# Products that nobody reads in TensorE's queue of an attention and experts kernel

## What is computed

```python
xn = _layernorm(x, axis=-1)
x = x + attn(xn, w_attn, w_proj) + ffn(xn, gate_w, gate_b, expert_bias, w1, b1, w2, b2)

# attn: 16 heads of 16, phi(a) = elu(a) + 1, causal, chunk by chunk of 128 rows
q, k, v = split(xn @ w_attn.T)
scores = where(tril, phi(q) @ phi(k).T, 0)
num = scores @ v + phi(q) @ S            # S: the sum of phi(k).T @ v of the chunks before
den = scores.sum(-1) + phi(q) @ z
y = num / (den + 1e-06);  attn = y @ w_proj.T

# ffn: each row goes to one of 8 experts
top_idx = argmax(xn @ gate_w.T + gate_b + expert_bias)
h = relu(xn @ w1[e] + b1[e])             # 256 -> 1024
y = h @ w2[e] + b2[e]                    # 1024 -> 256
```

## Time and profile before

| | |
|---|---|
| median of 3 executions | 514.7 us (514.43 to 514.87) |
| the profiled execution | 514.6 us |
| its span, first to last instruction | 512.8 us |
| mean granted clock of TensorE | 0.984 |
| TensorE products busy | 479.5 us, 94% of the span |
| VectorE, ScalarE, GpSimd busy | 406.6, 280.6, 259.5 us |
| longest waits of TensorE | 6.6 us for the first squared weights, 5.3 us for the first gathered rows |

### The profile page before, as it was taken

How to read it: one execution, slowest core, us unless ns; L and a number is a source line. 1 busy time by engine, 2 the same in 40 slices (tenths; PEclk the granted TensorE clock), 3 DMA queues, 4 the chain that set the end, 5 groups by cost and what they waited for, 6 DMA issues and landing times.

```text
span 512.8 us, 17442 instructions
## 1 busy us (share of the span) xinstructions
PE 479.5 (94%) x6067; PEld 393.1 (77%) x6067; DVE 406.6 (79%) x881; ACT 280.6 (55%) x537; POOL 259.5 (51%) x469
## 2 busy tenths in 40 slices
PE   1899999999999999999987599999999999999996
PEld 0678887888878888788864488888888888888884
DVE  3788999999999999999878377777777777776775
ACT  3448887788877888877875033333333333333331
POOL 4345667667667676676664523343343343333222
PEclk9999999999999999999999699999999999999998
DMA  8524565665655665655441522122212212210000
GB/s 254 202 65 139 184 204 155 188 206 173 190 179 171 190 201 171 193 177 177 138 159 63 184 57 79 56 82 75 65 54 71 79 58 76 71 49 28 24 15 1
DMA packets 34304, 62.88 MB, mean 123 GB/s; under 512 B 5677, under 2 KB 10030, under 8 KB 34096
## 3 DMA queue, kind: packets, MB, share of 16 engines
q1 hardware_dynamic: 29232, 49.17, 30.4%
q0 software_dynamic: 4992, 12.60, 8.1%
HBM read 51.00 MB, written 13.50 MB: 126 GB/s over the span
## 4 chain that ended last, share of the span: by engine, by line
PE 82%; DVE 5%; POOL 4%; issue 4%; ACT 3%; DMA 1%; DVEq 0%; POOLq 0%; ACTq 0%
PE ps L612 21%; PE ps L625 20%; PE ps L385 7%; PE ps L427 6%; PE ps L456 5%; PE ps L497 5%; PE ps L470 4%; PE ps L440 3%; PE ps L403 3%; PE ps L483 2%; PE ps L581 2%; PE ps L410 1%; PE ps L489 1%; PE ps L368 1%; DVE AR L664 1%
## 5 line engine op out<-in xcount | busy, mean ns | idle before, releaser
L612 PEld LDWEIGHTS ps<-AR,W 128*128 x1872 | 131.5, 99 | 40.0 <-issue 1.1
L612 PE MATMUL ps<-AR,W 128*128 128x128 f16 x1872 | 155.6, 221 | 0.9 <-ACT AR L1165 0.9
L625 PE MATMUL ps<-W,ST 128*128 x624 | 150.4, 326 | 0.0
L1174 ACT ACTIVATE ST<-ST 128x512 f16<-128x512 f32 x78 | 49.2, 630 | 116.3 <-DVE ST L1003 116.3
L1322 POOL DMA_INDIRECT out<-AR x39 | 39.5, 1013 | 118.6 <-DVE AR L1035 116.5
L1003 DVE SCALAR_TENSOR_TENSOR ST<-ps,TAs,B1S 128x512 f32<-128x512 f32 x78 | 58.6, 751 | 48.3 <-PE ps L612 48.3
L1261 POOL TENSOR_TENSOR W<-ST,W 128x512 f16<-128x512 f32 x64 | 74.2, 1160 | 28.9 <-ACT W L1117 28.3
L720 DVE TENSOR_TENSOR AR<-ps,CT 128x512 f32<-128x512 f32 x128 | 82.0, 683 | 3.9 <-PE ps L427 3.9
L1015 DVE SCALAR_TENSOR_TENSOR ST<-ST 128x512 f16<-128x512 f32 x78 | 53.6, 687 | 15.6 <-ACT ST L1174 15.6
L385 PE MATMUL ps<-xT,WA 128*128 128x128 f16 x768 | 50.7, 225 | 5.0 <-ACT xT L1067 2.7
L1317 POOL DMA_INDIRECT AR<-scr,AR x39 | 40.1, 1029 | 29.5 <-issue 21.6
(11 more groups left out here) (145 smaller groups left out, 757.9 us busy)
## 6 DMA issues: line engine op xcount, KB each, us to landing
ST<-in_w SPq DMA_DIRECT2D x128, 256.0 KB, 4.1
scr<-XR SPq DMA_DIRECT2D x32, 256.0 KB, 2.1
XR<-in_x SPq DMA_DIRECT2D x32, 128.0 KB, 4.6
AR<-in_b SPq DMA_DIRECT2D x1, 1024.0 KB, 4.8
AR<-in_wall SPq DMA_DIRECT2D x2, 388.0 KB, 4.1
AR<-scr,AR POOLq DMA_INDIRECT x39, 3.4
out<-AR POOLq DMA_INDIRECT x39, 2.5
ST<-in_cst SPq DMA_DIRECT2D x1, 576.0 KB, 5.2
```

The source lines that it names most:

```text
L612: a = e.matmul(dst, W[:, off:off + 57472][:, bass.ds(place_of(s), 128)], XT16[s % 2][:, xl * 256 + k * 128:xl * 256 + (k + 1) * 128], star ...
L625: a = e.matmul(PS[4 + s % 2][:, 0:w], src[h % 4][:, fs], W[:, off:off + 57344 + w][:, bass.ds(place_of(s), w)], start=(f == 0 and w == 512 ...
L1174: e.activation(HH[h % 4], H32[h % 2], ACT.Relu).then_inc(a_hh, 1)
```

## The change

Products of `one16` with itself, 128 columns each, are written into the unused columns of bank 6 and read by nobody. There are five groups: 64 ahead of the sums of squares, 36 behind them, 30 in step 1 between `xt(0)` and `qk(0)`, 20 in step 33 in front of `pr(29)`, behind a wait for VectorE's `t32(30)` (which reads the same bank), and 80 between the last product of the row numbers and the first transposes of gathered rows. 230 products in all, each with its weight load. Nothing is removed or moved, and no other engine's stream changes.

```diff
         def tensor(e):
+            def warm(n):
+
+                for _ in range(n):
+                    e.matmul(PS[6][:, 384:512], one16[:, :], one16[:, :], start=True, stop=True)
+
             e.wait_ge(p_one16, 1)
+            warm(64)
             for k in range(2):
                 ...
             a.then_inc(t_sq, 1)
+            warm(36)
...
                 if on(p - 1):
                     xt(p - 1)
+                if p == 1:
+                    warm(30)
                 mx(p)
...
                 if on(p - 1):
                     vg(p - 1)
+                if p == NC + 1:
+                    e.wait_ge(S["t32"], n_state(NC - 2))
+                    warm(20)
                 if on(p - 4):
                     pr(p - 4)
...
             a.then_inc(t_ids, 1)
+            warm(80)
```

## The result

The changed kernel takes 515.31 us (median of 20 executions, 514.68 to 516.39), the kernel of before 514.62 (20 executions beside them, 512.71 to 515.22). The ratio is 1.0017, 95% interval 1.0010 to 1.0025. It is slower by a little, where 1.2 us less was forecast. The profiled execution of the changed kernel is one of its shorter ones: 514.81 us, span 513.0. TensorE's busy time rose from 479.5 to 491.1 us, the mean granted clock from 0.984 to 0.989.

The account below looks back on a forecast made before the run. TensorE was taken to set the pace, wholly so in the expert stage, with gains only where it idles or runs at half rate. 0 + 0.2 + 1.0 = 1.2 us off gave 513.5 against 514.7, range 511.7 to 514.9.

Parts of the forecast that it names:

- What bounds the kernel: Whole kernel: TensorE busy nine tenths or more in long stretches, all 210.80 us of experts; time won ahead is kept.
- Part A: Beginning, 64, 36 and 30 products: clock down again when qk(1) starts, relu(0) still at 16.54; gain 0.
- Part B: End of attention, 20 products ahead of pr(29): clock holds past 267.8; 0.7 won less 0.5 on the ids, +0.2 us.
- The ids' price of 0.5: The 32 id products: clock may be lost ahead of them, costing up to 1.6 us more; 0.5 taken.
- its 0.7 us: End of attention: gain from the clock held past 267.8 that reaches the id products, +0.7 us.
- Part C: 80 products behind the ids: 2.1 us won by the clock, transposes 1.1 us late, net +1.0 us.
- 1.9 us (half of the 3.8 from 291.33 to 295) saved: First experts: full clock instead of half rate from 291.33 to 295 saves 1.9 us.
- queued behind the 80 is only `tx(0)`: Behind the 80 products: only tx(0) is queued, on which ACT's first copy and all experts wait; transposes 1.1 us late.
- no idle row ahead of `tx(0)`: First transposes of gathered rows: sign of the 80 products working, with tx(0) starting at 290 to 291.
- the first 48 products at 56 ns each: Start of the experts: sign of the 80 products working, the first 48 g1 products at 56 ns each.
- the slower one: Gathered rows: clock down through all 80 products, 3.2 us late, at most 2.1 back, B 0.5 more; 516.3, chance 0.08.
- the third rival: End of attention and ids: dull stretches trade places, B loses 0.7 to 1.5, C gives 0.8 to 1.0; 514.4 to 515.4, chance 0.17.

Follow-up runs that it names:

- e1: Kernel of before plus only the 130 products at the beginning (64, 36, 30): 516.02 us, ratio 0.9999 to before.
- e8: Changed kernel with expert 0's weights at a fixed address for the g1 products of the first two slots: 513.03 us, ratio 0.9988 to before.
- e12: Changed kernel with the load of the experts' numbers into registers ahead of the 80 products instead of behind them: 520.85 us, one execution.
- e5: The kernel of before again, unchanged, in the second job: 514.29 us, ratio 0.9998 to before.
- e4: Changed kernel without its 80 products behind the ids, first job: 514.88 us, ratio 0.9990 to before.
- e11: Kernel of before plus only the 130 products at the beginning, run again in the third job: 515.92 us, ratio 1.0002 to before.
- e2: Kernel of before plus only the 20 products in step 33, behind the wait for t32: 515.29 us, ratio 0.9993 to before.
- e3: Kernel of before plus only the 80 products behind the id products: 516.77 us, ratio 1.0014 to before.
- e9: The changed kernel again, unchanged, in the third job: 516.41 us, ratio 1.0021 to before.

## Why the prediction was wrong

- **What bounds the kernel.** Right in one half: 214.6 us of experts behind the first `g2`, kept whole (214.5 to 215.6 in the other profiles, 217.3 in e1's). It missed that the single profile was one draw. Before's executions spread over 2.5 us on its own chip; between its two profiles, 2.1 us apart, the difference comes from where the clock rises and falls. For the whole spread this isn't shown.
- **Part A, forecast 0.** The reason given held at `qk(0)`: relu(0) and the key transposes don't move (18.68 for 18.69), the gap became 2.91 us as worked out, `qk(1)` is back at half rate. Not foreseen: the transposes behind the gap were still at full rate, `qk(1)` started 0.46 us sooner (I had 20.8 unchanged), and the rise came in time to make it 0.78. That is no gain to count on either: e8 and e12 have the same products without it, and e5 has it without the products. The medians say 0.9999 and 1.0002, so the 0 holds as a median, but not for the reason given; how the 0.8 us of most profiles vanish in the median is not shown.
- **Part B, forecast +0.2.** `pr(29)` starts 0.49 us late against the pace of before (its distance to the projection before it is 8.40 us for 7.91), the clock holds past 267.8, the fall moves ahead of the ids: all as written. The ids' price of 0.5 was too high: all of them ran with the granted clock at 0.50 and took 2.65 us for 2.54. The fall is paid in the last projection instead (1.53 us for 1.13, 2.07 in e4). In the pair of profiles A and B together bring 1.55 us. What failed is the premise under it, that the fall at 267.8 belongs to the kernel. e5 and e11 have none. B insures against a fall that three of five profiles have, and its median of 0.9993 (e2), which can't be told from 1, is what is left of its 0.7 us.
- **Part C, forecast +1.0, the step that failed.** The length of the 80 was right: 6.1 us behind the ids, for 6.3 in the working. Two terms were wrong. "1.9 us (half of the 3.8 from 291.33 to 295) saved" measured 0.0: the first 78 `g1` products and two sets of transposes take 6.84 us at full clock and 6.86 in before, 3.8 of them at half clock, since the sequencer's addresses pace them at 81 ns (57 with fixed addresses, e8). And "queued behind the 80 is only `tx(0)`" overlooked the register load, 1.03 us in after, e3, e8 and e9, gone in e12. The first misled because the rows of before seem to bear it out: once the clock is up there, 30 `g1` products in a row start 56 ns apart (295.2 to 296.8). They stand behind a stretch at half clock, in which the settings of addresses come faster than the products need them; my reading is that they used up this lead, and the next ones are at some 82 ns again. What tells is the row of the settings, 16 in 1.9 us at half clock. Both terms were among the prediction's own signs: no idle row ahead of `tx(0)`, and the first 48 products at 56 ns each. With the two terms as measured, C is 0.2 for the transposes, less 1.1 for the products and 1.0 for the load: -1.9 us; the profiles give -1.5 to -1.7, or -0.7 to -0.9 where VectorE is late too.
- **The rivals.** The place of the slower one, products in front of the gathered rows, is where the time went. Its mechanism, a clock that stays down, is not what happened: the clock rose 6.8 us after its fall, 3.6 of them in the 80. The measured 515.31 lies inside the 514.4 to 515.4 of the third rival, nothing to be seen, but that is luck: it had C gain 0.8 to 1.0 and B lose, and it was C that lost.
- **What stays open.** The medians lie 0.7 us apart and the two profiles 0.2. e9's third fall of the clock is one way in which executions of the changed kernel can be worse than the profiled one. The mean granted clocks point to more slow stretches in most of them: 0.989 in seven of the 20, the profiled one among these, 0.985 or 0.986 in thirteen, and the nine slowest (515.65 to 516.39) all have 0.986. Where these fall isn't known without their profiles.

The Trainium skill, TensorE: Matmul & The Clock Gate (Part 1), says that the number of slow products at a start changes from run to run of one kernel. The runs agree: in before all 24 products of `qk(0)` and the six of `vg(0)` are slow (1.53 us), in e5 `vg(0)` takes 1.17 us. It is so for the falls too, which the page's sentence doesn't speak of: the same 1.75 us of idleness cost the clock in before and not in e5.

## What to carry to other kernels

Before paying for a full clock, look for what else paces the same instructions: products with addresses from registers may be paced by the sequencer, and the clock is then worth nothing. The pace of some products at full clock isn't enough, since they can live on a lead; count the settings of addresses beside them in a slow stretch, and see whether they come faster than the products will. Products put into a gap delay everything that the engine's stream does behind them in that gap, register loads too, which count as nobody's busy time; the view of their source line has them. And a gain or loss around a rise or fall of the clock needs the spread of many executions: one profile shows one draw. Of the versions run, the changed kernel without its 80 products is the best that is clear of no change, 0.9985 and 0.9990 in two jobs, with an interval clear of 1 in one of them.

## What was not expected of the hardware

The same kernel loses the clock behind 1.75 us of idleness in one execution and keeps it in another (0.50 and 1.00 granted in the stage behind it), worth 1.2 us on the way to the ids. The first `g1` products are paced at 81 ns by their addresses, between the 57 ns of e8 at full clock and the 105 ns at half. A load of eight registers takes 2.1 us on TensorE (1.03 of it shows behind a full queue, and 2.2 ahead of an empty one) and 0.85 us on VectorE. And VectorE's first expert step comes 9.8 to 9.9 us behind its tables in seven of the eight profiles of two jobs, where nothing recorded accounts for it, and within 8.1 us in the other job.
